# Where the middle weights of a binary convolution are made: GpSimd's six additions move from the convolution's start into the attention

## The reference

```python
# layer 0: attention with a residual
xn = group_norm(x)                                  # 32 groups
q, k, v = split(einsum('oc,bchw->bohw', qkv_weight, xn) + qkv_bias)   # 4 heads of 64
out = softmax(q k^T / 8) v                          # over the 4096 pixels
x = x + proj_weight @ out + proj_bias
# layer 1: two binary convolutions with a residual
def quantize_w1bit(w):                              # value: mean(|w|) * sign(w)
    return w + stop_gradient(mean(abs(w)) * sign(w) - w)
out = relu(batch_norm(x))                           # statistics over batch and pixels
out = conv3x3(out, quantize_w1bit(w0))
out = relu(batch_norm(out))
return conv3x3(out, quantize_w1bit(w1)) + x
```

## Time and profile before

| what | value |
|---|---|
| median of three runs | 2934.8 us |
| the profiled execution's own time | 2934.27 us |
| its span, first to last instruction | 2932.5 us |
| TensorE matmuls, busy | 2793.7 us (95%) |
| VectorE, busy | 2117.5 us (72%) |
| GpSimd, busy | 2027.3 us (69%) |
| ScalarE, busy | 1402.7 us (48%) |
| mean granted TensorE clock, share of full speed | 0.988 |
| output projection of batch 0 | about 1262 to 1294 us of the span |
| output projection of batch 1 | about 2518 to 2555 us |
| start of the convolutions | 2555.1 us |

### The profile page before, as it was taken

The page is one execution under the profiler, slowest core; times in us unless marked ns, Lnnn a source line. Parts: engine busy times, 40 slices in busy tenths (PEclk is TensorE's granted clock), DMA queues, the critical chain, the costliest instruction groups (busy, mean ns, idle before and its releaser), DMA issues. The chain is left out here.

```text
span 2932.5 us, 43630 instructions
## 1 busy us (share of the span) xinstructions
PE 2793.7 (95%) x17060; PEld 1013.2 (35%) x17060; DVE 2117.5 (72%) x2496; ACT 1402.7 (48%) x1477; POOL 2027.3 (69%) x1208
## 2 busy tenths in 40 slices
PE   5899999998999999998999999989999999799898
PEld 3333333333333333343333333343333333244343
DVE  5688888726777888456788888267777885588785
ACT  3355555553555555533555555534555555254342
POOL 2588888893888888844888888947888888500022
PEclk9999999999999999999999999999999999999999
DMA  5000000001000000041000000010000000421022
GB/s 213 35 1 1 1 1 1 1 5 60 1 1 1 1 1 1 1 153 42 1 1 1 1 1 1 1 44 1 1 1 1 1 1 1 148 79 60 15 100 86
DMA packets 26820, 78.27 MB, mean 27 GB/s; under 512 B 1921, under 2 KB 2177, under 8 KB 25601
## 3 DMA queue, kind: packets, MB, share of 16 engines
q1 hardware_dynamic: 25792, 74.19, 7.3%
q10 hardware_dynamic: 832, 1.45, 0.1%
HBM read 58.86 MB, written 16.78 MB: 26 GB/s over the span
## 5 line engine op out<-in xcount | busy, mean ns | idle before, releaser
L512 POOL TENSOR_TENSOR acc_pool<-acc_pool,prob 128x512 f32<-128x512 f32 (+1 forms) x992 | 1781.0, 1795 | 297.5 <-ACT prob L567 177.0
L803 DVE TENSOR_REDUCE m_part<-ps 128x2 f32<-128x1024 f32 x1024 | 1250.6, 1222 | 479.8 <-PE ps L662 456.0
L567 ACT ACTIVATE prob<-ps,exp_scale 128x1024 f32<-128x1024 f32 x1024 | 1086.9, 1111 | 1015.7 <-PE ps L719 1007.8
L703 PE MATMUL ps<-prob,vals 128*64 128x512 f32 x4096 | 990.9, 605 | 0.0
L662 PE MATMUL ps<-k_hi,q_hi 64*128 64x512 f16 x2048 | 394.3, 383 | 45.3 <-DVE m_part L803 45.3
L703 PEld LDWEIGHTS ps<-prob,vals 128*64 128x64 f32 x4096 | 248.7, 136 | 501.9 <-issue 364.2
L714 PE MATMUL ps<-q_hi,k_hi 64*128 64x512 f16 x2048 | 391.1, 379 | 0.0
L714 PE MATMUL ps<-q_hi,k_lo 64*128 64x512 f16 x2048 | 390.4, 378 | 0.0
L719 PE MATMUL ps<-m_rows,shift 64*128 64x512 f16 x2048 | 389.9, 377 | 0.4
L714 PE MATMUL ps<-q_lo,k_hi 64*128 64x512 f16 x2048 | 390.2, 378 | 0.0
L869 DVE TENSOR_TENSOR ps<-ps,prob 128x512 f32<-128x512 f32 x480 | 331.5, 691 | 72.4 <-ACT prob L567 72.4
(11 more groups left out here) (109 smaller groups left out, 1408.3 us busy)
## 6 DMA issues: line engine op xcount, KB each, us to landing
xt<-in_x SPq DMA_DIRECT2D x40, 512.0 KB, 4.3
xf<-in_x SPq DMA_DIRECT2D x4, 2048.0 KB, 16.5
x_scratch<-y_tile SPq DMA_DIRECT2D x16, 512.0 KB, 5.0
wf<-in_w_t SPq DMA_DIRECT2D x4, 1152.0 KB, 8.9
rows<-x_scratch SPq DMA_DIRECT2D x8, 576.0 KB, 5.3
rows<-x_scratch SPq DMA_DIRECT2D x8, 544.0 KB, 4.6
xn<-in_x SPq DMA_DIRECT2D x8, 512.0 KB, 5.6
xt<-x_scratch SPq DMA_DIRECT2D x4, 1024.0 KB, 5.1
```

The source lines that it names most:

```text
L512: nc.gpsimd.tensor_tensor(acc[:, part], acc[:, part], tile[:, part], ALU.add).then_inc(pool_add, 1)
L567: nc.scalar.activation(prob[:, n % PBUF], g.ps_s[:, kt % 2].rearrange("p h n -> p (h n)"), ACT.Exp, scale=g.exp_scale[:]).then_inc(exp_don ...
L703: last = mm(g.ps_o[own[h], :], vals[:, kt, own[h]], prob[:, n % PBUF, h * TB:(h + 1) * TB], start=(kt == 0), stop=(kt == KT - 1))
L803: v.tensor_reduce(m_part[:, block % 2, :, u], where[i] if where else g.ps_max, AX.X, ALU.max).then_inc(mx_used, 1)
```

## The change

The buffer wmid and its semaphore move to the top level. The three additions become a function, `middle_weights`. GpSimd calls it for both halves of the first convolution behind its last sum of batch 0, and at the start of the convolution block only for the second convolution. ScalarE makes the signs and sums of both halves behind batch 0's query blocks: after the first half it waits for its own absolute values and issues the load of the second half into wf itself. SP's wait and load of the second half are gone, and so is ScalarE's work on the second half at the end of batch 1.

```diff
--- before.py
+++ after.py
@@ -137,6 +137,7 @@
         signs0 = sb(top, "signs0", [P, CB, TAPS, C], F16)
         wf = sb(top, "wf", [P, TAPS * C])
         wsum = sb(top, "wsum", [P, 2, CB])
+        wmid = sb(top, "wmid", [P, 2, CB, 2, 3, C], F16)
         y_tile = sb(top, "y_tile", [P, 2, CB, TB])
         proj_w = sb(top, "proj_w", [P, CB, C])
         ones = sb(top, "ones", [P, P])
@@ -158,10 +159,11 @@
         proj_ready = sem("proj_ready")
         w_staged = sem("w_staged")
         wf_in, sign_done, wsum_ready = sem("wf_in"), sem("sign_done"), sem("wsum_ready")
+        wmid_step = sem("wmid_step")
 
         g = Shared()
         g.ps, g.ps_s, g.ps_max, g.ps_o, g.ps_misc, g.par, g.const = ps, ps_s, ps_max, ps_o, ps_misc, par, const
-        g.signs0, g.wf, g.wsum, g.y_tile = signs0, wf, wsum, y_tile
+        g.signs0, g.wf, g.wsum, g.y_tile, g.wmid, g.wmid_step = signs0, wf, wsum, y_tile, wmid, wmid_step
         g.y_out, g.w_staged, g.wf_in, g.sign_done, g.wsum_ready = y_out, w_staged, wf_in, sign_done, wsum_ready
         g.proj_w, g.ones, g.gn_a, g.gn_b, g.bound, g.fscale = proj_w, ones, gn_a, gn_b, bound, fscale
         g.exp_scale, g.qk_bias, g.proj_bias, g.bn_st, g.xt = exp_scale, qk_bias, proj_bias, bn_st, xt
@@ -178,6 +180,19 @@
             prologue(nc, x, qkv_t, proj_t, w0_t, par_d, const_d, g)
             attention(nc, x, qkv_t, w0_t, x1_d, g)
         convolutions(nc, x1_d, w1_t, out, g)
+
+
+def middle_weights(nc, pool, g, signs, l, c):
+
+    pool.wait_ge(g.sign_done, l * CB + c + 1)
+    g0, g1, g2 = (signs[:, c, 3 * i:3 * (i + 1), :] for i in range(3))
+    plus, minus = g.wmid[:, l, c, 0], g.wmid[:, l, c, 1]
+    base = (l * CB + c) * 3
+    nc.gpsimd.tensor_tensor(minus, g0, g2, ALU.add).then_inc(g.wmid_step, 1)
+    pool.wait_ge(g.wmid_step, base + 1)
+    nc.gpsimd.tensor_tensor(plus, minus, g1, ALU.add).then_inc(g.wmid_step, 1)
+    pool.wait_ge(g.wmid_step, base + 2)
+    nc.gpsimd.tensor_tensor(minus, minus, g1, ALU.subtract).then_inc(g.wmid_step, 1)
 
 
 def sign_weights(nc, act, g, signs, layer, c):
@@ -452,10 +467,6 @@
                     for s in range(2):
                         load(x, b, n2 * 2 + s, s, n2 * 2 + (before + 1 + s))
                         store(b, (n2 - 1) * 2 + s, s)
-                if b < B - 1:
-
-                    sp.wait_ge(g.wsum_ready, b + 1)
-                    sp.dma_start(g.wf[:], w0_t[b + 1]).then_inc(g.wf_in, 16)
                 for s in range(2):
                     store(b, NB - 2 + s, s)
 
@@ -532,6 +543,9 @@
                         split_k(b, hp, NB // 2 - 1, s)
                     for qb in range(NB):
                         sums(pair * NB + qb)
+                if b == 0:
+                    for c in range(CB):
+                        middle_weights(nc, pool, g, g.signs0, 0, c)
 
         @block.scalar
         def _(act):
@@ -610,7 +624,12 @@
                         if qb == NB - 2 and it0 + NB < 2 * B * NB:
                             normalize_first((b * 2 + hp + 1) // 2, 1 - hp)
                         softmax(it0 + qb, qb == 0, qb == NB - 1)
-                sign_weights(nc, act, g, g.signs0, 0, b)
+                if b == 0:
+                    for c in range(CB):
+                        sign_weights(nc, act, g, g.signs0, 0, c)
+                        if c + 1 < CB:
+                            act.wait_ge(g.wsum_ready, c + 1)
+                            act.dma_start(g.wf[:], w0_t[c + 1]).then_inc(g.wf_in, 16)
 
         @block.tensor
         def _(pe):
@@ -950,7 +969,7 @@
         parts = sb("parts", [P, 2, CB, 2, 4, CR // 2, PW], F16)
         hid = sb("hid", [P, CB, B, N])
         signs1 = sb("signs1", [P, CB, TAPS, C], F16)
-        wmid = sb("wmid", [P, 2, CB, 2, 3, C], F16)
+        wmid = g.wmid
         half1 = sb("half1", [P, CB, TB])
         mid = sb("mid", [P, CB, 2, TB])
         cs = sb("cs", [P, 2, 4])
@@ -970,7 +989,7 @@
         small = sem("bn_small")
         bvar_ready, bstd_ready, bn_ready = sem("bvar_ready"), sem("bstd_ready"), sem("bn_ready")
         wsum_mm, scale_ready = sem("wsum_mm"), sem("scale_ready")
-        wmid_step = sem("wmid_step")
+        wmid_step = g.wmid_step
         rows_in = [[sem(f"rows_in{s}{c}") for c in range(CB)] for s in range(2)]
         relu_done = sem("relu_done")
         zero_rows = sem("zero_rows")
@@ -1040,18 +1059,8 @@
             edges = parts[:].rearrange("p s c h k r w -> p (s c h k r) w")
             nc.gpsimd.memset(edges[:, :, 0:1], 0.0).then_inc(border, 1)
             nc.gpsimd.memset(edges[:, :, PW - 1:PW], 0.0).then_inc(border, 1)
-            for l in range(2):
-
-                for c in range(CB):
-                    pool.wait_ge(g.sign_done, l * CB + c + 1)
-                    g0, g1, g2 = (signs[l][:, c, 3 * i:3 * (i + 1), :] for i in range(3))
-                    plus, minus = wmid[:, l, c, 0], wmid[:, l, c, 1]
-                    base = (l * CB + c) * 3
-                    nc.gpsimd.tensor_tensor(minus, g0, g2, ALU.add).then_inc(wmid_step, 1)
-                    pool.wait_ge(wmid_step, base + 1)
-                    nc.gpsimd.tensor_tensor(plus, minus, g1, ALU.add).then_inc(wmid_step, 1)
-                    pool.wait_ge(wmid_step, base + 2)
-                    nc.gpsimd.tensor_tensor(minus, minus, g1, ALU.subtract).then_inc(wmid_step, 1)
+            for c in range(CB):
+                middle_weights(nc, pool, g, signs1, 1, c)
 
             for k in range(B * BLOCKS):
                 b, q, _, _ = where(k)
```

## The result

The changed kernel takes 2929.39 us (median of 16 runs, 2927.24 to 2931.84) against 2934.9 us for the kernel before (16 runs, 2933.73 to 2936.96): 5.5 us less. The ratio is 0.9981 with a 95% interval of 0.9973 to 0.9988, so it is faster. Whether by more than 0.2% (5.9 us) the measurement leaves open. The forecast was 2928.6 us in a range of 2927.4 to 2931.0.

A forecast was written before the change was run, and what follows sets the result against it. TensorE bounds attention; at the first convolution's start, tiny VectorE batch norm instructions held by GpSimd's additions set the end. Gains of 6.2 + 0 + 0 + 0 = 6.2 us from 2934.8 gave 2928.6 us, range 2927.4 to 2931.0.

The forecast's parts named there:

- Step 1: Start of the first convolution: six GpSimd additions leave, batch norm's VectorE chain runs free, first relu comes 6.2 us earlier.
- The naive sum: Convolution start: the five VectorE durations, 8.34 us against 0.95 in layer 1, a 7.4 us gain if nothing else is late.
- Step 2: Batch 0's output projection: the six additions run beside VectorE work of kinds not held; cost nothing, at most 9.8 us.
- Step 3: Batch 0's output projection: ScalarE loads the second half and makes its signs early, in idle time; cost nothing.
- Step 4: Batch 0's residual loop: the moved load runs beside four transfers, covered by 2 us; cost nothing, bound 1.2 us.
- A: Convolution start: the rows' load lands 5 to 7.4 us after issue, gain only 5.2 to 2.8 us; chance 0.26.
- B: Batch 0's output projection: GpSimd's additions hold VectorE there too, price up to 9.8 us, 2938.4 us; chance 0.04.
- C: Batch 0's output projection: the load holds ScalarE past the next projection, costing 4.5 us, 2933.1 us; chance 0.02.
- D: Convolution start: VectorE's hold isn't GpSimd's work, the chain stays slow, no change at 2934.8 us; chance 0.03.

The follow-up runs named there:

- the rows there: Changed kernel with the first block's first load of rows left out, the first relu reading a buffer already there (other data): 2929.56 us.
- the second pair: The changed kernel and the kernel before, each measured once more with nothing edited: 2929.72 us (11 runs) and 2936.37 us (10 runs).

## Why the prediction was right, point by point

**Sign, mechanism and size.** It forecast 6.2 us; the joint gave 6.1 in the profile and 6.2 in the second, the medians 5.5 and 5.9. The run with the additions back has the old joint and the old time, so the gain is that of the six additions' place. The medians are the coarser measure: two kernels above with the same joint to 0.1 us (14 additions; memsets late) lie 6.5 and 6.4 us under the kernel before, and the mean of the four is 6.1. That the forecast time came within 0.8 us is in part luck, since it rests on one profile and three runs of the kernel before, and single profiles of it differ by 2.7 us.

**Step 1** held term by term. The memset keeps the first instruction until about 1.0 us (stated: up to 1.1). The shift came 3.8 us behind the first aggregation, so within the 3.6 to 4.0 that 2558.8 to 2559.2 mean. The load was last by 0.4 us, in the second profile by 0.3, and landed after 4.21 and 4.1 us where 4.0 was taken. The naive sum, 7.4 us, would have been 1.3 us too much. The runs with late memsets and with the rows there confirm that these two limits, and not a third, made the difference.

**Step 2** held: the cover isn't slack but the kind of instruction and operand, and 14 additions cost as little as six.

**Step 3** held with more slack than said, since the load landed after 6.1 us, not 8.9.

**Step 4** had its result right and its margin wrong. I had the four transfers through 2.3 us ahead of the residual that needs the last of them. In the profile after, that last transfer, a store, goes out at 1274.67 and lands 7.0 us later where it took 4.6 before:

```profile
L445 SPq DMA_DIRECT2D x_scratch<-y_tile x1: 1430/1430/1430, 1274.7 to 1274.7; - x1
...
DMA to landing us min/median/max: 7.0/7.0/7.0
```

So at 1281.7, 1.0 us before the residual at 1282.71. The rule from the Trainium skill, "DMA: Bandwidth & Descriptors", on arbitration between queues that take turns, agrees with this as far as it goes: SP's four transfers landed 2.4 to 2.8 us later than before, beside the load on ScalarE's queue, which landed after 6.1 us. In which order the packets went no view here shows. Nothing waited for these four. The idle time of the residuals on stores wasn't as unchanged as said: 5.3 us in this profile and 4.0 in the second, against 4.6 and 4.5 before, so no cost is told from chance.

**The rivals.** A is real but rarer than given: of eight profiles with this load at its old place, seven have it at 4.0 to 4.3 us, and the one with 6.1 wasn't the changed kernel. B, C and D are excluded by the runs above and by the 18 us that ScalarE idles. The chance of 0.63 for more than 0.2% was somewhat high: the measured 5.5 us lies under that line and the second pair's 5.9 on it, since with a gain of 6.1 us the spread of the attention decides.

**A sign of being wrong that misled.** The prediction said that a span gain below 5 us with the relu on time would mean a loss at batch 0. The span gain was 3.2 us with the relu on time, and no loss of that size was there: the difference stands ahead of batch 0's output projection, from one execution to another.

## What to carry to other kernels

Where tiny VectorE instructions take a microsecond and more, lay GpSimd's timeline beside them: if they end where GpSimd's instructions end, the two take turns, and no chain of waits will say so. GpSimd's additions were free beside VectorE's scalar_tensor_tensor with one input in PSUM, its statistics, its reciprocals and its tensor_tensor with one input in PSUM. A tensor_scalar, or a tensor_tensor with two SBUF inputs, took up to 1.5 us longer for each addition in its way. Move such work to a stretch of the first kind rather than behind the wait. When a stall of several microseconds goes, look for what landed unseen behind it, and take away the two nearest limits together before saying that a limit doesn't matter.

## What the runs showed that I had not expected

The same program's attention stage varies by 2.7 us from one execution to the next, in part by TensorE's pace at its first matmuls (eight equal ones in 5.06 and 5.74 us; 6.69 in the changed kernel); this hides a joint that is fixed to 0.2 us. GpSimd pays for the lock as well: its additions took 1.96 to 2.08 us instead of 1.64 where VectorE's two-input operations ran beside them. And an issue of a DMA on SP's queue took 1.43 us instead of 0.39 when ScalarE's load of 1152 KB and three transfers were under way, without any wait of the program; in the other nine profiles with this load it took 0.91 to 1.58.

Not every GpSimd instruction holds every such VectorE instruction. The memset, which reads nothing, held the variance's tensor_scalar (1.01 us instead of 0.17). In the version with all four loads early it runs beside VectorE's first combinations, which have two SBUF inputs, and they take 1.29 us a pair, as in the changed kernel, where no memset is beside them. GpSimd, then VectorE:

```profile
2561.25 1.57 POOL L1078 MEMSET parts<- 128x256 f16 x1
...
2561.82 1.29 DVE L1241 TENSOR_TENSOR comb<-early 128x512 f32<-128x512 f32 x2 [1.31 <-ACT early L1102]
```
